# A transformer block with two cross-attentions: another order of work ahead of its first loop, with matmuls on zeros between the first real ones

## What is computed

```python
x = x + _L0_xattn_ref(_layernorm(x), ctx, ctx, Wq, bq, Wk, bk, Wv, bv, Wo)
    # HEADS = 16, HEAD_DIM = 8
    q = (xq @ Wq.T + bq)...; k = (xk @ Wk.T + bk)...; v = (xv @ Wv.T + bv)...
    scores = jnp.einsum('bhnd,bhmd->bhnm', q, k) * scale
    weights = jax.nn.softmax(scores, axis=-1)
    out = jnp.einsum('bhnm,bhmd->bhnd', weights, v)
    return out.transpose(0, 2, 1, 3).reshape(B, N, EMBED) @ Wo.T
x = x + _L0_ffn_ref(_layernorm(x), ...)      # quantised gated layer
x = x + _L1_xattn_ref(_layernorm(x), ctx, ...) # slot attention, 3 iterations
x = x + _L1_ffn_ref(_layernorm(x), ...)      # 8 experts, summed
```

## Time and profile before

| | us |
|---|---|
| median of 3 runs | 779.32 |
| lowest, highest | 776.95, 780.71 |
| the profiled execution | 777.27 |
| its span in the trace | 775.5 |

### The profile page before, as it was taken

One profiled execution on the slowest core, in us unless ns is written; L12 is line 12 of the kernel. 1 busy time (PEld: TensorE's weight loads), 2 busy tenths in 40 slices (PEclk: granted clock), 3 DMA queues, 4 the chain that ended last, 5 costly groups with the idle time before them and its releaser, 6 DMA issues.

```text
span 775.5 us, 23846 instructions
## 1 busy us (share of the span) xinstructions
PE 673.7 (87%) x8894; PEld 484.3 (62%) x8894; DVE 586.3 (76%) x1100; ACT 529.0 (68%) x1153; POOL 450.0 (58%) x486
## 2 busy tenths in 40 slices
PE   5789999999999999997743868899888788899997
PEld 2257776777777777775521467788877676444443
DVE  5878888887777777889788566888888887755663
ACT  3267777767677777775473398999999884455554
POOL 1666777777777777781100033667776973466664
PEclk9799999999999999999985978989999889999999
DMA  6535444444444444331400602640644441002100
GB/s 191 153 88 174 133 127 118 122 135 139 139 139 130 133 128 132 94 103 19 168 28 0 246 2 84 239 175 10 241 167 165 167 165 43 0 2 81 42 0 25
DMA packets 26721, 86.16 MB, mean 111 GB/s; under 512 B 5829, under 2 KB 7493, under 8 KB 26645
## 3 DMA queue, kind: packets, MB, share of 16 engines
q1 hardware_dynamic: 26264, 84.73, 34.4%
q10 hardware_dynamic: 384, 0.46, 0.2%
HBM read 65.19 MB, written 0.46 MB: 85 GB/s over the span
## 4 chain that ended last, share of the span: by engine, by line
PE 49%; DVE 15%; ACT 14%; POOL 10%; issue 8%; SPq 2%; DMA 1%; POOLq 0%; DVEq 0%; ACTq 0%
PE ps L1493 10%; POOL ctx_lo L675 9%; PE ps L1510 8%; PE ps L1524 8%; ACT c_prob L840 7%; PE ps L1480 4%; PE ps L1751 3%; PE ps L1469 3%; DVE tile_max L935 3%; PE ps L1733 2%; ACT w0T L840 2%; PE ps L1529 2%; ACT merge_w L840 2%; DVE amax_part L1151 1%; SPq L510 1%
## 5 line engine op out<-in xcount | busy, mean ns | idle before, releaser
L935 DVE TENSOR_REDUCE tile_max<-ps 128x1 f32<-128x500 f32 x336 | 214.6, 675 | 49.5 <-PE ps L1493 48.9
L701 ACT ACTIVATE probs<-ps 125x896 f32<-125x896 f32 x192 | 175.3, 916 | 92.8 <-PE ps L1510 92.0
L1493 PE MATMUL ps<-k_hi,qdiag 128*128 128x500 f16 x336 | 129.8, 389 | 6.2 <-DVE tile_max L935 3.2
L840 ACT ACTIVATE c_prob<-ps,c_bias,row_scale 125x56 f32<-125x56 f32 x384 | 118.8, 547 | 7.9 <-DVE c_bias L1239 7.9
L1510 PE MATMUL ps<-qstack,kstack 98*125 98x224 f16 x768 | 106.7, 262 | 0.4
L630 POOL TENSOR_TENSOR c_prob<-c_prob,c_weight 125x672 f32<-125x672 f32 x32 | 43.1, 1347 | 101.9 <-DVE c_weight L1253 101.7
L675 POOL TENSOR_TENSOR ctx_lo<-ctx_hi,ctx_lo 128x448 f16<-128x448 f32 x64 | 70.2, 1098 | 53.3 <-ACT ctx_lo L876 53.3
L1510 PEld LDWEIGHTS ps<-qstack,kstack 98*125 98x125 f16 x768 | 86.3, 137 | 21.1 <-ACT probs L701 2.8
L1733 PE MATMUL ps<-query_hi,ctx_hi 128*128 128x56 f16 x576 | 54.8, 193 | 28.8 <-ACT c_prob L840 20.8
L1524 PE MATMUL ps<-probs,v_aug 125*32 125x168 f32 x1536 | 74.8, 312 | 3.3 <-ACT probs L701 2.5
L572 POOL TENSOR_TENSOR qstack<-q_rep,slot_mask 96x224 f16<-96x224 f32 (+1 forms) x64 | 33.7, 556 | 75.3 <-PE ps L1510 70.3
(11 more groups left out here) (278 smaller groups left out, 1707.2 us busy)
## 6 DMA issues: line engine op xcount, KB each, us to landing
row_tiles<-in_ctx_rows_wide SPq DMA_DIRECT2D x40, 774.0 KB, 5.7
ctx<-in_ctxT SPq DMA_DIRECT2D x16, 750.0 KB, 5.2
rows_in<-in_ctx_rows SPq DMA_DIRECT2D x16, 750.0 KB
kstack<-k_hi SPq DMA_DIRECT2D x128, 93.8 KB, 2.8
kstack<-k_lo SPq DMA_DIRECT2D x64, 93.8 KB, 2.7
ctx_hi<-in_wg SPq DMA_DIRECT2D x8, 256.0 KB, 2.7
ctx_hi<-in_wu SPq DMA_DIRECT2D x8, 256.0 KB, 3.1
ctx_hi<-in_wd SPq DMA_DIRECT2D x8, 256.0 KB, 3.6
```

Source lines behind the costliest of these rows:

```text
L701: nc.scalar.activation(probs[c % RING_P][0:CH, :].rearrange("p (k w) -> p k w", k=2), score_tile(c)[0:CH], ACT.Exp, scale=float(HD) ** -0. ...
L840: last = nc.scalar.activation(c_prob[n % PROBS][:, c, :], ps[0:CH, 2 * (n % 2) + c // 6, bass.ts(c % 6, TOK)], ACT.Exp, bias=c_bias[n % 2] ...
L935: nc.vector.reduce_max(tile_max[:, u % MAXT, u // MAXT:u // MAXT + 1], ps[:, MAXB + (u + p) % 2, 0:KCOLS], AX.X).then_inc(max_done, 1)
L1493: nc.tensor.matmul(ps[:, MAXB + (u + p) % 2, 0:KCOLS], qdiag[p][:, bass.ts(t, 128)], k_hi[p][:, bass.ts(j, KCOLS)], start=True, stop=True) ...
```

## The change

- PE: a tile `warm` of zeros (128x512, fp16) is multiplied with itself 12 times ahead of the means, 5 times behind them, and 8 times between the variances and the spreading. The result goes to a bank that isn't read.
- DVE: one more memset for `warm`, counted on `magic_ready`; the reciprocal stands ahead of `split_weights`; `k_low(0, 0, j)` move back by one place each, and the third goes behind the first two maxima.
- ACT: the root's table is asked for first of all; the queries stand ahead of the second `k_high`; the third is moved between the two halves of the `q_rep` DMAs; `exp(0, 0)` and `exp(0, 1)` go ahead of `k_high(1, 1, 0)` and `(1, 1, 1)`.
- PE: `keys(0, 0)` behind the spreading, `keys(0, 1)` behind the queries, `keys(0, 2)` behind the first two maxima; `scores(0, 0, 0)` and `(0, 0, 1)` ahead of `keys(1, 0)` and of the first maximum of batch 1; `values(0, f)` at steps 4, 6, 8 in place of 7, 9, 11.

```diff
-        FIRST_VALUES = {7: 0, 9: 1, 11: 2}
+        FIRST_VALUES = {4: 0, 6: 1, 8: 2}
...
+            act.wait_ge(ready, 1)
+            load_table(ACT.Sqrt)
             context_high(0)
             act.wait_ge(ready, 3)
             layernorm_sd(0)
             act.wait_ge(constants, 1)
             k_high(0, 0, 0)
-            k_high(0, 0, 1)
             for i in range(2):
                 act.wait_ge(q_ready, i + 1)
                 nc.scalar.activation(q_hi[:, bass.ts(i, HALF)], ps[:, i, 0:HALF], ACT.Identity,
                                      bias=bias_qkv[:, 0:1]).then_inc(q_hi_done, 1)
-            k_high(0, 0, 2)
+            k_high(0, 0, 1)
             act.wait_ge(q_hi_done, 2)
             for r in range(2):
+                if r:
+                    k_high(0, 0, 2)
...
+            exp(0, 0)
             k_high(1, 1, 0)
+            exp(0, 1)
             k_high(1, 1, 1)
...
-            main(0, 0)
+            main(0, 0, 2, 2)
...
+            nc.vector.memset(warm[:], 0.0).then_inc(magic_ready, 1)
...
-            layernorm(0, split_weights, lambda: k_low(0, 0, 0))
-            k_low(0, 0, 1)
+            layernorm(0, None, split_weights)
+            k_low(0, 0, 0)
...
-            k_low(0, 0, 2)
+            k_low(0, 0, 1)
...
                 maxima(0, 0, step_units(FIRST_STEPS, c))
+                if c == 0:
+                    k_low(0, 0, 2)
...
-            def first_keys():
-                pe.wait_ge(constants, 1)
-                keys(0, 0)
-
+            def warm_up(n):
+
+                for _ in range(n):
+                    nc.tensor.matmul(ps[:, MAXB + 1, 0:512], warm[:, 0:128], warm[:], start=True, stop=True)
+
+            pe.wait_ge(magic_ready, 1)
+            warm_up(12)
             pe.wait_ge(first_params, 16 * len(first_list))
-            layernorm(0, None, first_keys)
-            keys(0, 1)
+            layernorm(0, lambda: warm_up(5), lambda: warm_up(8))
+            pe.wait_ge(constants, 1)
+            keys(0, 0)
...
-            keys(0, 2)
+            keys(0, 1)
...
                 maxima(0, 0, second)
+                if c == 0:
+                    keys(0, 2)
...
+            scores(0, 0, 0)
             keys(1, 0)
+            scores(0, 0, 1)
             maxima(1, 1, range(1))
             keys(1, 1)
...
-            main(0, 0)
+            main(0, 0, done=2)
```

More of the change, by code:

```diff
@@ L134, in build @@
         magic = sbuf("magic", [128, 2])
+        warm = sbuf("warm", [128, 512], F16)
         sd = sbuf("sd", [128, GW])
@@ L745, in _, with main @@
                     load_table(ACT.Exp)
+            exp(0, 0)
             k_high(1, 1, 0)
+            exp(0, 1)
             k_high(1, 1, 1)
-            def main(b, p, batches=2):
+            def main(b, p, batches=2, done=0):
                 for c in range(NCH):
-                    exp(b, c)
+                    if c >= done:
+                        exp(b, c)
                     if c in KEYS_AT and KEYS_AT[c][0] <= batches:
@@ L800, in _ @@
             last = F0 - 1
-            act.wait_ge(magic_ready, 1)
+            act.wait_ge(magic_ready, 2)
             act.wait_ge(scale_done, 3)
@@ L1559, in _, with main @@
             maxima(1, 1, range(1, UNITS_AHEAD))
-            def main(b, p, batches=2, also=None):
+            def main(b, p, batches=2, also=None, done=0):
                 for c in range(NCH):
-                    scores(b, p, c)
+                    if c >= done:
+                        scores(b, p, c)
                     if c == AHEAD and batches:
```

## The result

| | before | after |
|---|---|---|
| median of 20 runs, us | 778.10 | 780.79 |
| lowest, highest | 775.12, 782.27 | 777.56, 783.61 |
| the profiled execution | 777.27 | 778.79 |
| its span | 775.5 | 777.0 |

The ratio is 1.0032 with a 95% interval of 1.0018 to 1.0045: slower by 2.7 us, where 2 us less was forecast. One more set of 12 runs of the same kernel, later, gave 1.0006 (0.9987 to 1.0026), so the loss is small and its size isn't firm. That the kernel did not get the gain is firm: the forecast was a ratio of 0.9974, outside both intervals.

What follows compares the result with a forecast made beforehand. PE was taken as the bound from the loop's start, so the change should start the dense stretch earlier: -3.2 + 0.75 + 0.5 = -1.95, 777.27 to 775.3, or 777.3 us against the median; range 774.0 to 780.8.

Steps and rivals of the forecast that it cites:

- A, the norm: Kernel start up to the first maximum: earlier root and reciprocal and a spreading at the higher clock give -3.2 us.
- B, the maxima: The 21 maxima of batch 0: moved third key part costs, earlier values partly repay; +0.75 us, bounds -0.6 and +2.2.
- C, from the maxima to the third scores: Last reduction of batch 0 to the third scores: +0.5 us, bounds 0 and +2.5.
- The order: Between maxima and third scores: `exp(0, 0)` in front of `k_high(1, 0)` delays it from +2.27 to +3.45, costing +1.2 us.
- The clock: Between maxima and third scores: `keys(1, 1)` may run at the high clock, 0.83 instead of 1.45, giving -0.65 us.
- the bound: Maxima to third scores, worst case: clock low when the dense stretch begins, PE itself the bound; +2.5 us.
- Rival 1: Clock stays high all through, by zero matmuls over the norm and earlier values over the maxima: -3.3, 776.0 us; chance 0.22.
- Rival 2: In the norm, POOL's subtraction holds up the reciprocal, which begins at 12.77, not 11.7: +1.05, 778.3 us; chance 0.08.
- Rival 3: Warming does not take; clock low at variances and spreading, zero matmuls pure load: +3, 782.3 us; chance 0.08.
- Its mild form: The 8 zero matmuls themselves raise the clock in time for the spreading: sum about 0, 779.2 us; chance 0.12.
- Rival 4: The head start is eaten later, by a DMA or by POOL: 779.3 us; chance 0.1.
- The rest of the span behind the third scores: Work behind the third scores is unchanged and 727 us long, so what that mark gains, the end gains.

Runs made afterwards that it cites:

- e17: The changed kernel run once more without an edit; median 780.34 us, ratio 1.0006 to the kernel before.
- e8: e1 without its zero matmuls, so early table, reciprocal ahead of the weights and moved keys are left; 778.60 us, ratio 1.0002.
- e12: e1 with values early (steps 4, 6, 8) and zero matmuls in PE's gaps from the last maximum to the loop; 775.46 us, ratio 0.9972.
- e3: The changed kernel with only the values back at steps 7, 9, 11, scores still early; 780.61 us, ratio 1.0018.
- e9: The kernel before with only the first two scores and exponentials of batch 0 moved early; 782.02 us, ratio 1.0027.
- e5: The changed kernel with more zero matmuls (fills) in PE's gaps from the last maximum of batch 0 to the loop's first steps; 777.76 us, ratio 0.9977.
- e1: The changed kernel with batch 0's scores and exponentials back in the loop and values back at steps 7, 9, 11; 777.49 us, ratio 0.9972.
- e6: e5 with ACT's two `k_high` of batch 1 each ahead of the exponential they stood behind; 777.69 us, ratio 0.9983.
- e16: The kernel before with only zero matmuls added in PE's gaps from the last maximum to the loop; 779.77 us, ratio 0.9998.
- e7: e1 with zero matmuls in PE's gaps from the last maximum of batch 0 to the loop; 777.37 us, ratio 0.9984.
- e15: The changed kernel with more zero matmuls only between the first scores and the loop's third step; 779.50 us, ratio 0.9994.
- e14: The changed kernel with more zero matmuls only at the shift, 6 ahead and 5 behind; 780.01 us, ratio 1.0004.

## Why the prediction was wrong

The forecast was 2 us less, and the kernel got slower. The range, 774.0 to 780.8, still holds the 780.79, by its allowance for noise and by luck: slower had a chance of 0.05.

**A, the norm: right.** Forecast: first maximum at 20.3, 3.2 earlier. Measured 21.06 with the context 0.74 late, and 20.29 in e17. The steps were right one by one: means at the higher level without use by themselves, table load gone, reciprocal right behind the root, spreading 1.78 for 1.8. e8 adds what the prediction left open: without the warming it is 0.3 and not 3.2.

**B, the maxima: right within its bounds.** Forecast +0.75 (-0.6 to +2.2). Measured +0.2, with the clock at 0.50 from 27.0 to 30.4, and, in e17 and e12 with the clock high all along, -0.7. The `k_low` behind the second reduction is there (23.03, next reduction at 23.69).

**C, from the maxima to the third scores: the step that failed.** Forecast +0.5, with +2.5 as the bound; measured +3.36, and 12.02 - 9.53 = +2.49 in e17. The term had two parts, and the runs size both:

- *The order*: forecast +1.2, `k_high(1, 0)` at +3.45. Measured with the clock high, +3.42 to +3.44 (e3, e9, e5) against +2.23 (e1), 1.2 again. The size was right, the cause only half: I blamed `exp(0, 0)` in front of `k_high`, and taking it away gives back 0.2 (e6), because PE has a cost of nearly the same length beside it. `keys(1, 0)` had run before while DVE copied the shift (40.12 beside 40.23), and now waits behind `scores(0, 0, 0)` for that copy. My own section on the change had the wait, and I priced only the ACT side of it.
- *The clock*: forecast -0.65, as a credit, since `keys(1, 1)` might run at the higher level. Measured: before lost 0.63 to it (10.72 in e16 against 11.35), which agrees with the credit; but the changed kernel loses 15.32 - 12.15 = 3.17 in one trace and 1.8 in the other. So the credit was a debit of 1.2 to 2.5.

To the third scores the split is: 1.43 for the order with e5's fills in the loop (10.33 in e5 less 8.90 in e1), 12.89 - 10.33 = 2.56 for the clock, less 0.63 that before had lost (9.53 - 8.90), is 3.36; in e17 1.43 + 1.69 - 0.63 = 2.49. These terms are differences of the same marks, so they add up by construction; that the middle one is the clock rests on e5, where the fills take the low stretches away. The failed term is so the clock's: put at -0.65, it was, up to the third scores, +1.9 in one trace (2.56 - 0.63) and +1.1 in the other. Why the clock fell I could have asked of the trace of before. There, scores stood at 44.77 and 47.08, in the holes that the four reductions of batch 1 leave PE. I moved them ahead and did not ask what would fill the holes: nothing did, PE waited 1.71 us in one piece, and the loop began at 0.50. The early values did the same at the end of the maxima. The prediction named this as its bound ("if the clock is low when the dense stretch begins") and as what would show it wrong, but took it for unlikely without looking at what would be left in the holes.

**The rivals.** Rival 1 (clock high all through, -3.3) did not come by itself; made by fills and with the scores left in the loop, e12, it gives -4.2 at the fourth scores. Rival 2 is out: the reciprocal took 1.55 from 12.54, beside POOL's subtraction of 10.49 to 13.52. Rival 3 had the direction and nearly the price (+3 for +2.7), but at another place: the warming of the norm did take, and the low clock came at the shift and the loop's start. Its mild form, the 8 zero matmuls at the lower level, turned up in two of the thirteen profiled executions with the 8 zero matmuls (3.19 us in e7, 3.14 in e15, 1.90 in the others). Rival 4 is near the truth in words, a head start eaten later, but neither a DMA nor POOL ate it.

The Trainium skill (TensorE: Matmul & The Clock Gate, Part 1) warns that the number of slow matmuls differs from run to run of one kernel and that one shouldn't fit to a count. The traces agree: the 8 zero matmuls took 1.90 or about 3.15 us with nothing changed in front of them, and the two traces of the changed kernel have low stretches of 7 and 3.4 us at the shift.

**The marks and the time.** The rest of the span behind the third scores was 727.4, as foretold (727), and 731.9 in e17. Behind the fourth scores it runs from 723.5 (e12) to 730.0 (e17) over the traces, though the work there is the same. It is longer where the clock is low for longer later on: behind the fourth scores the stretches at 0.50 sum to 70 us in e12 and to 87 in e17, and over the 18 traces each microsecond of them goes with about 0.3 us of that rest (correlation 0.89). None of the experiments touches those stretches, so this part of a single execution's time is scatter beside the change. Over the 17 traces other than before's, the fourth scores' gain and the gain in the ratio go together loosely (correlation 0.65), about 0.4 us of the second for 1 us of the first; e15, late in its trace by 4.1 us, has a ratio of 0.9994.

**What stays open.** How large the loss of the change is (1.0032 and 1.0006, intervals that overlap), how it splits between the two falls of the clock (e14 and e15 can't be told apart in time), and why a head start of 4 us at the loop is worth 2 at the end; that the mark is from one execution and the ratio from twelve may be part of it.

## What to carry to other kernels

Work that is moved ahead leaves its old place empty: look at which engine used it to fill a wait, and what the granted clock does there afterwards. When work is put in front of the bound, put the start of the longest chain first (here the next batch's keys), and never behind a wait which that chain doesn't need. Where a matrix engine has to wait in the ramp to a dense loop, spend matmuls on zeros in all of the gaps, since with half of them filled the clock fell in the other half here, and keep each batch shorter than its gap at the lower clock.

## What the runs showed of the hardware

- The clock fell ahead of stretches in which PE was far from idle: it was busy 4.15 of 6.50 us before the fall at 37.3, with no wait above 1.41 us near it, and 0.96 of 2.90 before the one at 47.5.
- Matmuls on zeros raise and hold the granted clock: the 12 from 1.22 us on let the means run in 1.77 in place of 3.33 us (e8), and with fills from 36.4 us on it stayed at 1.00 over the shift and the loop's start in e5.
- Fills are not free once the clock is down: five of 256 columns took 1.27 us in place of 0.71.
- DVE's reciprocal on 128x224 was not held up by POOL's subtraction beside it (1.55 us as before), while the copy to fp16 of 128x128 had been: 3.02 us, against 0.16 at 14.01 in the changed kernel, when the subtraction was over.
